# The sync engine's store of an early normalised row tile, moved to the end of its step in the attention loop of a two-layer transformer kernel

## What is computed

```python
x = x + xattn(layernorm(x), ctx, ctx, mask)       # the "band" part
h = layernorm(x)
for l in range(2):                                # the part that the change touches
    q, k, v = split(shift_token(h) @ wqkv[l])     # q, k normalised per head, scaled, rotated
    h = h + local_attention(q, k, v) @ wo[l]      # 8 heads of 64, windows of 256
    t = shift_token(h)
    t = (t - mean(t)) / sqrt(var(t) + 1e-5) * ln_g[l] + ln_b[l]
    a, g = split(t @ w1[l] + b1[l])               # 2 x 1365 columns
    h = h + (a * gelu(g)) @ w2[l] + b2[l]
x = x + h
```

## Time and profile before

| what | us |
|---|---|
| median of 3 runs | 2985.37 (2982.37 to 2986.47) |
| the profiled execution, its own time | 2983.97 |
| its span in the trace, first to last instruction | 2982.2 |
| PE busy in the span | 2900.1 (97%) |
| DVE, ACT, POOL busy | 2073.7, 1343.1, 1327.9 |
| mean granted clock of PE | 0.99 of full speed |

### The profile page before, as it was taken

One profiled execution on the slowest core, in us unless ns is written; L12 is line 12 of the kernel. 1 busy time (PEld: TensorE's weight loads), 2 busy tenths in 40 slices (PEclk: granted clock), 3 DMA queues, 4 the chain that ended last, 5 costly groups with the idle time before them and its releaser, 6 DMA issues. The chain is left out here.

```text
span 2982.2 us, 53002 instructions
## 1 busy us (share of the span) xinstructions
PE 2900.1 (97%) x20256; PEld 2545.1 (85%) x20256; DVE 2073.7 (70%) x4135; ACT 1343.1 (45%) x2807; POOL 1327.9 (45%) x1406
## 2 busy tenths in 40 slices
PE   9999998899999999999999999899999999999999
PEld 7887887688889899999998887778888899999998
DVE  8977776666767666766656767657666767666765
ACT  7875655455554222222235555546555322222222
POOL 7857766667641111222205666666662222222221
PEclk9999999999999999999999999999999999999999
DMA  6752222322147777776683232322217777777775
GB/s 222 234 188 92 96 100 89 107 90 77 40 152 285 257 266 271 258 264 254 254 315 104 93 107 89 106 93 85 72 46 274 256 256 276 272 283 282 265 275 192
DMA packets 184480, 547.01 MB, mean 183 GB/s; under 512 B 26262, under 2 KB 82074, under 8 KB 161700
## 3 DMA queue, kind: packets, MB, share of 16 engines
q1 hardware_dynamic: 184084, 543.56, 51.2%
q10 hardware_dynamic: 144, 0.07, 0.0%
HBM read 447.11 MB, written 93.70 MB: 181 GB/s over the span
## 5 line engine op out<-in xcount | busy, mean ns | idle before, releaser
L1241 PE MATMUL quad<-fhT_f,slot_f 128*128 128x256 f32 (+1 forms) x2088 | 596.8, 286 | 0.2 <-DVE sums_f L2055 0.2
L1242 PE MATMUL quad<-fhT_f,slot_f 128*128 128x256 f32 (+1 forms) x2088 | 590.2, 283 | 0.0
L1243 PE MATMUL quad<-fhT_f,slot_f 128*128 128x256 f32 (+1 forms) x2088 | 589.9, 283 | 0.0
L1241 PEld LDWEIGHTS quad<-fhT_f,slot_f 128*128 128x128 f32 (+1 forms) x2088 | 392.9, 188 | 1.6 <-DVE sums_f L2055 0.8
L1242 PEld LDWEIGHTS quad<-fhT_f,slot_f 128*128 128x128 f32 (+1 forms) x2088 | 393.0, 188 | 0.0
L1243 PEld LDWEIGHTS quad<-fhT_f,slot_f 128*128 128x128 f32 (+1 forms) x2088 | 392.8, 188 | 0.0
L1660 ACT ACTIVATE gate_f_raw<-gate_f_raw,bias_f 128x512 f32<-128x512 f32 (+1 forms) x176 | 127.1, 722 | 576.6 <-DVE gate_f_raw L2078 576.6
L1528 ACT ACTIVATE lprob<-lprob,small 128x384 f32<-128x384 f32 (+2 forms) x512 | 288.5, 565 | 179.7 <-DVE small L1879 179.7
L2163 POOL TENSOR_SCALAR stats<-stats 128x1 f32<-128x1 f32 x64 | 43.5, 679 | 708.7 <-DVE stats L2018 708.0
L2280 POOL TENSOR_TENSOR turned_qk<-with_cos,with_sin 128x256 f32<-128x256 f32 x252 | 185.8, 758 | 325.3 <-DVE with_sin L1903 250.9
L995 PE MATMUL bank_pair<-wqkv_h,hT 128*128 128x512 f32 x992 | 318.6, 402 | 0.0
(11 more groups left out here) (296 smaller groups left out, 7439.4 us busy)
## 6 DMA issues: line engine op xcount, KB each, us to landing
slot_f<-parts SPq DMA_DIRECT2D x160, 1792.0 KB, 7.6
slot_f<-parts SPq DMA_DIRECT2D x16, 1190.0 KB, 5.2
s_in<-stream SPq DMA_DIRECT2D x128, 128.0 KB, 2.8
s_res<-stream SPq DMA_DIRECT2D x64, 256.0 KB, 2.9
stream<-a_out SPq DMA_DIRECT2D x64, 256.0 KB, 2.0
res_f<-stream SPq DMA_DIRECT2D x63, 256.0 KB, 7.3
h_in_f<-stream SPq DMA_DIRECT2D x112, 128.0 KB, 6.6
parts<-part_high SPq DMA_DIRECT2D x20, 512.0 KB, 2.6
```

Of the source, the lines that this page charges most:

```text
L1241: e.matmul(bank[0:n, :], high, row_high, start=c == 0, stop=False)
L1242: e.matmul(bank[0:n, :], high, row_low, start=False, stop=False)
L1243: ins = e.matmul(bank[0:n, :], low, row_high, start=False, stop=c == 1)
```

## The change

In SP's attention loop the wait for `ln_normed` and the store of the early tile leave the block ahead of the inner loop and go into the inner loop at its last pass, p = 3, ahead of the store of `a_out`. No instruction is added or taken away, and no other engine's program changes. The early load (`early_in`) stays where it is.

```diff
                     w.wait_ge(S("norm_sum"), base + s)
                     wait_stored(l, "ffn", i)
                     load_shifted(A.square[:, 0, :], 2 * l + 1, i, S("early_in"))
-                    w.wait_ge(S("ln_normed"), base + i + 1)
-                    load(early_dram[l][i * P:(i + 1) * P, :], A.square[:, 1, :], S("early_store"))
                 for p in range(PAIRS):
                     if p == 0 and prepared_item(s, 2) is not None:
                         store_parts(l, prepared_item(s, 2), False)
...
                     if p == 2 and prepared_item(s, 1) is not None:
                         store_parts(l, prepared_item(s, 1), True)
+                    if p == PAIRS - 1 and i is not None:
+                        w.wait_ge(S("ln_normed"), base + i + 1)
+                        load(early_dram[l][i * P:(i + 1) * P, :], A.square[:, 1, :], S("early_store"))
                     if (s, p) == (TILES - 1, PAIRS - 1):
```

## The result

The changed kernel took 2932.39 us as the median of 4 runs (2932.03 to 2932.76), the kernel before 2984.9 us (2982.37 to 2986.47) beside it: a ratio of 0.9825, 95% interval 0.9808 to 0.9842. The forecast was 2939.0, range 2932.0 to 2949.0, so the time lies inside it by 0.4 us only: the gain is 52.5 us where 46.3 were worked out. The spans of the two profiled executions differ by 2982.2 - 2930.9 = 51.3 us.

The account below looks back on a forecast made before the run. PE was taken to be held by POOL, late because SP's parts stores and loads stood behind the early tile; 23.50 + 22.77, together 46.3 us, off 2983.97 gave 2937.7, set on the median 2939, range 2932 to 2949.

Parts of the forecast that it names:

- What bounds the kernel: SP waits for DVE's early tile, so parts loads, POOL's additions and PE's transposes come late: 37.1 us of PE waits.
- The two parts stores and three loads: Step 12, SP's queue: no longer behind the early tile, loads at 429.9, landed 433.8; POOL's 9.17 us wait becomes none.
- What a step gets back: Steps 13, 15, 17, 19 shrink to their peers' lengths: 23.50 us in layer 0, 22.77 in layer 1, together 46.3.
- The clock: PE behind the longest wait ran at 0.50 of full speed for 5.53 us; this goes with the idle time.
- The second way to the sum: PE: waits of 37.1 us plus 10.3 of extra busy time, 47.4, less roughly 1 us of peers' idling.
- The early store: SP, early steps: still issued at 435.26; ACT's square 0 to 0.8 us a step better, effect on PE 0.
- The rule against the change: SP's queue: increments land after earlier writes, so loads still writing would delay the early store; loads landed 1.5 us ahead.
- The first: Rival: ACT's wait for the early store replaces POOL's, all 25.6 us stay on the path, 2964.7 us; chance 0.08.
- The second: Rival: `part_low` or `parts_out` come as late as `ln_normed`, so SP's order does not matter, 2985 us; chance 0.02.
- The third: Rival: early store ends up behind the loads at SP's last pass, steps 12 to 18: 3032 us; chance 0.03.
- The range: 2932 to 2949 us: 6 down for ACT, 8 up for 1 us left per step, half of the 4 us spread each way.
- The signs: Right: SP's eight waits about 4 us, PE's 37.1 vanish; wrong: ACT wait above 4, PE idle at L1111 not for POOL.

Follow-up runs that it names:

- the graded loads: Changed kernel's parts loads moved behind the early store, behind the a_out store too, or into the next step: 2950.96, 2961.08 and 2980.36 us.
- the store from ACT's queue: Changed kernel, but ACT instead of SP waits for the early tile and issues its store ahead of its square: 2931.54 us, repeated 2931.75.
- the late store alone: Changed kernel with only the early tile's wait and store moved into the next step, behind its loads: 2966.5 us, ratio 0.9941.
- the run in which only the wait stayed: Kernel before with SP's wait for the early tile in place, its store moved to the step's end behind parts stores and loads: 2983.52 us.
- the kernel with the loads behind the a_out store: Changed kernel with the early steps' three parts loads issued last, behind the early store and the a_out store: 2961.08 us, ratio 0.9927.

## Why the prediction came out as it did

**What bounds the kernel: right.** SP's order is the cause, shown by the graded loads and by the store from ACT's queue. The chain that the prediction gave from the loads to PE was one of two: next to POOL's `divide(t, 1)` there is ACT's rounding and DVE's split. It named the second only as something that "moves up with them".

**The two parts stores and three loads: right.** Predicted for step 12 were loads at 429.9, issued by 431.4, landed 433.8, POOL's wait none. Measured, after taking off the 0.5 us by which this whole execution lies later: 429.1, 430.6, and 434.7, which is 0.9 later than worked out and left POOL a wait of 0.28. The term that was off is the 3.9 us to landing, from one step of the kernel before: it was 5.6 here (3.7 to 5.8 over the eight steps). POOL was to be 2.0 us early at the transposes; in step 13 its division ended 1.4 us ahead of them. A wait of 0.2 us for DVE's maxima stands there, as in the undisturbed steps.

**What a step gets back: the term that was mis-sized.** It was "the length of its peer, since peers have the same instructions": 46.3. The windows that I compared do not have the same instructions. The prediction had itself noted the longer busy time of step 19 "for less work". In the earlier trace rows step 13 holds 146 matrix instructions and its peer, step 5, holds 158; step 19 holds 106 and step 11 holds 114. The early tile's DVE work pushes `add_residual`, the mark, back by 0.75 us in the early step, while PE goes on; the window of the next step then starts that much later in PE's work. Windows over pairs of steps put it right. First the kernel before, steps 12 and 13 and their peers 4 and 5:

```profile
415.26:461.88 46.62, 42.32 (x294) 34.55 (x295) 32.17 (x75) 24.65 (x55) 29.36 (x28) 0.96 0.28 96
253.11:294.04 40.93, 40.73 (x294) 33.10 (x296) 29.82 (x71) 24.61 (x55) 29.50 (x26) 1.00 0.29 97
```

Then the changed kernel, steps 12 and 13:

```profile
415.73:456.67 40.94, 40.74 (x294) 33.08 (x296) 32.67 (x76) 24.37 (x55) 30.69 (x28) 1.00 0.33 110
```

With 294 matrix instructions in each, the pair costs 5.69 us more than its peer before and 0.01 us after. So the steps behind the early ones came out at 20.4 and not at the 21.2 that the prediction named. Over all eight pairs, each against the pair eight steps earlier, which has the same count of matrix instructions, the kernel before is 51.8 us longer. These are the 46.3 of the prediction and 5.5 by which the early steps themselves are longer than their peers (0.63 to 0.79 each), which the prediction left out. The changed kernel is 1.3 us longer than its peers, most of it in the two pairs of steps 18 and 19. The 50.5 between are the gain, up to what lies outside these steps.

**The clock: right in kind, too small.** The second way to the sum gave 10.3 us of extra busy time on PE, from the same unequal windows; over the pairs it is 15.5. (The 1 us that it then took off for the idle time of the peers' PE is 2.3 in the earlier trace rows, of which 1.2 stand in the steps behind the early ones as well.) PE's busy time fell by 2900.1 - 2884.4 = 15.7 us over the span: with the 37.1 us of waits 52.8, against 51.3 of span.

**The early store: right.** It goes out with DVE's last instruction as before, ACT waits for it as before, and PE does not. The sum's bounds of 0 to 0.8 us a step better held with 0. The experiments add how narrow this is: issued some 3 us later it costs 34 us.

**The rule against the change: not decisive here, and in agreement with two runs.** The early store's landing took 2.0 us at the median in the kernel before and in the changed kernel. Where the parts loads were issued right ahead of it (the run in which only the wait stayed) it took 3.1, and behind the next step's row loads 3.2; in all 16 steps of these two runs it landed 0.6 to 0.8 us behind the last load issued ahead of it. That agrees with the rule that the Trainium skill gives in "DMA: Bandwidth & Descriptors", section "Queues, rings and completion order", though traffic shared by the DMA engines would show the same. In the changed kernel the loads had landed before the store went out, by 0.3 to 2.7 us over the eight steps, where the prediction had 1.5.

**The rivals.** The first (ACT's wait takes POOL's place, 2965) did not happen: 26.6 us of that wait stand there at no cost. The second (no effect) did not either. The third's place and condition were right, as the late store alone shows, but its price was not: with POOL late as well the total is 2983.5, not 3032, because the delays overlap; alone it is 2966.5.

**The range: hit by luck.** Its own terms, 6 us down and 2 for the spread, give 2931 at the lower end and not the 2932 stated. The 6 us stood for the early store landing sooner, which gained nothing; what brought the time there was the length of the peers, for which the range had no room below. The changed kernel once more took 2931.56, which is outside the stated range (the kernel before beside it was 0.9 us lower as well).

**The signs.** SP's waits for the early tile fell to 4.2 us on average and 5.0 at most, as named, and ACT's stayed under 4. POOL's waits for raw weights were to lose eight of 13 pieces and lost three, the others being short. PE idle at the transposes for something other than POOL was named a sign of being wrong. The view has 7.2 us in 23 such pieces for DVE (5.8 in 16 before), but in the steps behind the early ones they are 0.2 us each, so that it was no sign.

## What to carry to other kernels

On a queue that issues many DMAs in order, look for the wait that ends last and list what stands behind it that could go now; who waits for those is where the time is, here a third engine whose first instruction held back two others. When a step is compared with an undisturbed one, compare the counts of instructions in the two windows first; if they differ, the mark itself has moved, and the window must be widened until they agree. Two delays in one step that start from the same event are not added up: make each late alone before giving a price to both.

## What the runs showed of the hardware that was not expected

The matrix engine's clock can fall behind an idle time as short as 1.8 us, and need not fall behind one of 3.1. In the kernel with the loads behind the a_out store, PE's transposes waited in step 13 and in step 17 of layer 0 for almost the same time:

```profile
451.99 1.50 PE L1114 MATMUL quad<-ident,lprob 128*128 128x128 f32 x12 [2.47 <-POOL lprob L2274]
...
542.53 2.79 PE L1114 MATMUL quad<-ident,lprob 128*128 128x128 f32 x12 [2.39 <-POOL lprob L2274]
```

The windows of the two steps, with the columns of the earlier trace rows:

```profile
435.81:458.54 22.73, 20.26 (x146) 16.40 (x144) 15.68 (x36) 13.30 (x29) 16.28 (x15) 1.00 0.34 116
...
526.40:550.67 24.27, 21.88 (x148) 18.07 (x146) 15.15 (x36) 13.52 (x29) 16.42 (x15) 0.93 0.32 109
```

And the second set of transposes alone:

```profile
542.53:545.32 2.79, 2.79 (x13) 2.79 (x14) 0.06 (x1) 0.81 (x1) 2.71 (x4) 0.50 0.00 0
```

Behind 2.47 us the clock stayed at 2.4 GHz and the twelve transposes took 1.50 us; behind 2.39 us they ran at 1.2 GHz all the way and took 2.79, and the step is 1.5 us longer. The two ends of what the runs show are step 17 of layer 0 with the early store alone late, whose clock column is 0.93, and step 15 of layer 1 with the loads behind the a_out store, whose column is 1.00:

```profile
537.11 0.93 PE L997 MATMUL bank_pair<-wqkv_h,hT 128*128 128x512 f32 x2 [1.82 <-DVE with_sin L1905]
...
1875.41 1.50 PE L1114 MATMUL quad<-ident,lprob 128*128 128x128 f32 x12 [3.06 <-POOL lprob L2274]
```

In the kernel before the clock column of all eight steps with a wait is below 1.00, 0.93 or 0.94 down to 0.81. So a removed wait returned more than its own length: 37.1 us of waiting were worth 51.3.
